# Local attention prepared two units earlier, and gated convolution as a rolling program over sequences

## The reference

```
xz = xn @ in_w.T + in_b
xi, z = jnp.split(xz, 2, axis=-1)
xc = conv1d(xi, conv_w, 4 taps, causal, one filter per feature) + conv_b
xc = _silu(xc)
xp = xc @ xproj_w.T
C = xp[..., 1 + D_STATE:]
gate = jax.nn.sigmoid(jnp.mean(C, axis=-1, keepdims=True))
y = xc * gate + D * xc
y = y * _silu(z)
y = y @ out_w.T + out_b
return y + residual
```

```
q, k, v = split(shift_token(x) @ wqkv)          # to heads
q = l2norm(q) * qs;  k = l2norm(k) * ksc
q, k = rotary_xpos(q, k)
sim  = einsum('bhwid,bhwjd->bhwij', bq, bk)     # bk, bv: this window and the last
attn = softmax(where(mask, -max, sim))
out  = einsum('bhwij,bhwjd->bhwid', attn, bv)
x = x + o @ wo                                  # a gated feed-forward follows
```

## Time and profile before

| | |
|---|---|
| median of 3 runs | 8063.11 us (8062.08 to 8072.71) |
| the profiled execution | 8073.38 us, its span 8071.7 us |
| PE busy | 5969.8 us (74%) |
| DVE busy | 4107.3 us (51%) |
| ACT busy | 2971.3 us (37%) |
| POOL busy | 1953.7 us (24%) |
| gated convolution | about 800.6 to 1000.1 us of the span |
| local attention, four times | 5220.5 to 5702.5, 5800.6 to 6281.0, 6879.0 to 7366.0, 7465.5 to 7949.8 us |

### The profile page before, as it was taken

The page is one execution under the profiler, slowest core; times in us unless marked ns, Lnnn a source line. Parts: engine busy times, 40 slices in busy tenths (PEclk is TensorE's granted clock), DMA queues, the critical chain, the costliest instruction groups (busy, mean ns, idle before and its releaser), DMA issues. The chain is left out here.

```text
span 8071.7 us, 121471 instructions
## 1 busy us (share of the span) xinstructions
PE 5969.8 (74%) x45848; PEld 2884.3 (36%) x45848; DVE 4107.3 (51%) x6441; ACT 2971.3 (37%) x6472; POOL 1953.7 (24%) x1781
## 2 busy tenths in 40 slices
PE   5557567786768876666678999877777798678677
PEld 3445151114442222222234544434344333344343
DVE  4333435662427745888844444344444566444444
ACT  1002323553334541444311222345355355354453
POOL 0113032212142201444511000034143011341341
PEclk6558676887888888787785887889899888899888
DMA  1001012211121100000003221111111000110110
GB/s 44 4 30 51 14 62 68 65 49 64 48 62 43 37 16 14 0 0 0 0 7 64 52 52 44 26 41 38 31 40 38 9 1 1 47 40 15 51 39 23
DMA packets 261161, 268.98 MB, mean 33 GB/s; under 512 B 113600, under 2 KB 190656, under 8 KB 258688
## 3 DMA queue, kind: packets, MB, share of 16 engines
q1 hardware_dynamic: 250368, 240.26, 11.5%
q0 software_dynamic: 10240, 21.25, 0.8%
HBM read 122.59 MB, written 71.66 MB: 24 GB/s over the span
## 5 line engine op out<-in xcount | busy, mean ns | idle before, releaser
L2170 PE MATMUL ps<-s_l2b_hc,ident 128*128 128x512 f32 x512 | 361.4, 846 | 332.6 <-DVE s_l2b_hc L2333 332.6
L1942 DVE TENSOR_REDUCE s_l3l_negmax<-ps 128x4 f32<-128x512 f32 x256 | 175.0, 683 | 744.0 <-PE ps L1783 744.0
L2118 POOL TENSOR_TENSOR s_l2b_Bx<-s_l2b_du,s_l2b_B 128x512 f32<-128x512 f32 x256 | 406.5, 1610 | 473.3 <-ACT s_l2b_B L2240 410.4
L1873 ACT ACTIVATE s_l3l_probs<-ps,s_l3l_biases,s_l3l_q_inverse 128x128 f32<-128x128 f32 x1024 | 455.6, 462 | 55.7 <-DVE s_l3l_biases L1944 55.3
L2325 DVE TENSOR_TENSOR_SCAN s_l2b_state<-s_l2b_decay,s_l2b_Bx 128x512 f32<-128x512 f32 x256 | 389.9, 1562 | 154.6 <-ACT s_l2b_decay L2246 113.3
L1721 POOL TENSOR_TENSOR s_l3l_probs<-s_l3l_probs,s_l3l_inverse 128x512 f32<-128x512 f32 x256 | 266.9, 1043 | 830.5 <-DVE s_l3l_inverse L1923 830.3
L1745 PE MATMUL ps<-s_l3l_hs,s_l3l_wqk 128*128 128x512 f32 x512 | 305.0, 703 | 177.3 <-DVE s_l3l_prod L1897 95.5
L1057 DVE TENSOR_REDUCE s_L3a_negmax<-ps 128x1 f32<-128x128 f32 (+3 forms) x512 | 236.1, 488 | 362.0 <-PE ps L893 359.5
L638 DVE TENSOR_REDUCE s_L1a_negmax<-ps 128x1 f32<-128x512 f32 x512 | 316.5, 681 | 153.3 <-PE ps L501 152.6
L1035 ACT ACTIVATE s_L3a_pt<-ps 128x256 f32<-128x256 f32 (+3 forms) x512 | 195.3, 434 | 530.3 <-PE ps L893 528.5
L908 PE MATMUL ps<-ks,s_L3a_qs 40*128 40x256 f32 (+3 forms) x1024 | 360.2, 610 | 30.1 <-DVE s_L3a_kvsq L1072 16.5
(11 more groups left out here) (658 smaller groups left out, 13547.7 us busy)
## 6 DMA issues: line engine op xcount, KB each, us to landing
s_l3l_qk<-s_l3l_rope SPq DMA_DIRECT2D x1024, 64.0 KB
scratch_rope<-s_L3a_rope SPq DMA_DIRECT2D x32, 512.0 KB, 2.8
ks<-scratch_parts SPq DMA_DIRECT2D x384, 32.0 KB
s_L3a_qs<-scratch_rope SPq DMA_DIRECT2D x64, 128.0 KB
ks<-scratch_rope SPq DMA_DIRECT2D x64, 128.0 KB
s_L0e_slots<-scratch_sent SPq DMA_DIRECT2D x16, 396.0 KB, 5.9
s_L1e_slots<-scratch_sent SPq DMA_DIRECT2D x16, 396.0 KB, 6.3
scratch_square<-s_L1a_rows SPq DMA_DIRECT2D x24, 256.0 KB, 3.0
```

What stands on the lines that cost most here:

```text
L1873: act.activation(t["probs"][:, U % (LAG + 1), k, :], ps[:, U % 2, P * k:P * (k + 1)], ACT.Exp, bias=t["biases"][:, U % (LAG + 1), k:k + 1] ...
L2118: pool.tensor_tensor(t["Bx"][:, n % 2, k, :], t["du"][:, b % 2, k, :], t["B"][:, n % 2, :], ALU.mult).then_inc(s["bx_ready"], 1)
L2170: pe.matmul(ps[:, 4 + k, :], g["ident"][:, :], t["hc"][:, n % 2, k, :], start=(n == 0), stop=(n == STATES - 1)).then_inc(s["summed"], 1)
```

## The change

Two stages are rewritten, the rest is as it was.

**Local attention.** The preparation runs two units earlier (`EARLY = 2`): units 0 to 5 of sequence b take what units 2 to 7 took, and units 6 and 7 take the first two items' units of sequence b+2. Before the first scores, the whole first sequence and two units of the second are prepared (`FIRST`). Two v items change places (the third v now comes with the norms). The signal of the DMAs is split in two, `q_stacked` and `k_stacked`, so that POOL waits only for the half whose rows it overwrites.

```
+    EARLY = 2
     def prep(b, u):
-        if b == BATCH:
+        if not 0 <= b < BATCH:
             return []
...
         if u == 4:
-            return [("norm", b), ("v", b, 1)]
+            return [("norm", b), ("v", b, 3)]
         if u == 5:
-            return [("v", b, 0), ("v", b, 3)]
+            return [("v", b, 0), ("v", b, 1)]
...
+    def beside(b, u):
+        u += EARLY
+        return prep(b + 1 + u // UNITS, u % UNITS)
+    FIRST = [item for u in range(UNITS) for item in prep(0, u)] + [item for u in range(EARLY) for item in prep(1, u)]
...
-                sp.wait_ge(s["stacked"], START + b * STACKED)
+                sp.wait_ge(s["q_stacked"], START + b * STACKED)
+                sp.wait_ge(s["k_stacked"], START + b * STACKED)
...
-                pool.wait_ge(s["stacked"], START + b * STACKED)
+                pool.wait_ge(s["q_stacked" if e < 2 else "k_stacked"], START + b * STACKED)
...
-                    if u < 4 and b + 1 < BATCH:
-                        rotate(b + 1, u)
-                    if u == 4 and b + 2 < BATCH:
+                    for ahead, e in ((b + 1, u + EARLY), (b + 2, u + EARLY - UNITS)):
+                        if 0 <= e < 4 and ahead < BATCH:
+                            rotate(ahead, e)
+                    if u == 3 and b + 2 < BATCH:
                         shift(b + 2)
```

```
+            for b in range(BATCH):                                     # POOL
+                pool.tensor_tensor(x[:, cols], x[:, cols], h[:, cols], ALU.add).then_inc(s["added"], 1)
...
+            for b in range(BATCH):                                     # PE
+                gates(b)
+                if b + 2 < BATCH:
+                    project_x(b + 2)
+                if b:
+                    outputs(b - 1)
+                if b + 1 < BATCH:
+                    project_z(b + 1)
+            outputs(BATCH - 1)
...
+            pad(0); pad(1); gate_rows(0)                               # ACT
+            for b in range(BATCH):
+                for k in range(2):
+                    act.activation(t["xc"][:, b % 2, k, :], t["conv"][:, b % 2, k, :], ACT.Silu).then_inc(s["xc_ready"], 1)
+                act.activation(t["gate"][:, b % 2, :], ps[:, 6, :], ACT.Tanh).then_inc(s["gate_ready"], 1)
+                if b + 2 < BATCH:
+                    pad(b + 2)
+                if b + 1 < BATCH:
+                    gate_rows(b + 1)
...
+            convolution(0)                                             # DVE
+            vec.tensor_copy(t["gate_w"][:, :, :], ps[:, 7, 0:2 * P].rearrange("p (k c) -> p k c", k=2)).then_inc(s["gate_copied"], 1)
+            for b in range(BATCH):
+                if b + 1 < BATCH:
+                    convolution(b + 1)
+                gated(b)
+                if b:
+                    add_out(b - 1)
+            add_out(BATCH - 1)
```

More of the change, by code:

```diff
@@ L1431, in gated_convolution @@
 def gated_convolution(nc, g, w):
[L1434 to L1437, removed]
@@ new lines, in outputs @@
+            def outputs(b):
+                pe.wait_ge(s["halved"], START + 1)
+                pe.wait_ge(s["done"], START + b)
+                for k in range(2):
+                    pe.wait_ge(s["y_ready"], START + 2 * b + k + 1)
+                    mm = pe.matmul(ps[:, 7, :], t["out_w"][:, k, :], t["y"][:, b % 2, k, :], start=(k == 0), stop=(k == 1))
+                mm.then_inc(s["out_ready"], 1)
+            project_x(0)
+            for k in range(2):
+                mm = pe.transpose(ps[0:16, 6, k * P:(k + 1) * P], t["c_w"][:, k, :], g["ident"][:, :])
@@ new lines, in _ @@
+            mm.then_inc(s["c_turned"], 1)
+            project_x(1)
+            pe.wait_ge(s["rows_copied"], START + 1)
+            pe.wait_ge(s["pads_set"], START + 1)
+            for k in range(2):
+                mm = pe.matmul(ps[:, 7, k * P:(k + 1) * P], t["c_rows"][:, k, :], t["thirty_second"][:, :], start=True, stop=True)
+            mm.then_inc(s["gate_made"], 1)
+            project_z(0)
+            pe.wait_ge(s["gate_copied"], START + 1)
+            for b in range(BATCH):
[6 more added lines that the diff above has]
+                    project_z(b + 1)
@@ L1516, in _, with gated @@
-                            own(ins, *((s["conv_done"], b * 2 + k + 1) if tap == 3 else ()))
+                            ins = vec.scalar_tensor_tensor(out=conv, in0=shifted, scalar=weight, in1=conv, op0=ALU.mult, op1=ALU.add)
+                            own(ins, *((s["conv_done"], 2 * b + k + 1) if tap == 3 else ()))
+            def gated(b):
                 vec.wait_ge(s["gate_ready"], START + b + 1)
+                if b > 1:
+                    vec.wait_ge(s["out_ready"], START + b - 1)
@@ L1713, in _ @@
             shift(1)
+            for e in range(EARLY):
+                rotate(1, e)
             shift_values(0)
@@ L1811, in values @@
                 mm.then_inc(s["pv_done"], 1)
-            for u in range(UNITS):
-                for item in prep(0, u):
-                    side(item)
+            for item in FIRST:
+                side(item)
             for U in range(BATCH * UNITS + BEHIND):
@@ L1826, in _ @@
                 if b < BATCH:
-                    for item in prep(b + 1, u):
+                    for item in beside(b, u):
                         side(item)
```

139 lines of the change are left out of this document (73 added, 66 removed).

## The result

The changed kernel takes 7727.1 us (median of 4 runs, 7723.0 to 7739.2) against 8067.9 us for the kernel before: a ratio of 0.9578, interval 0.956 to 0.9595, so 341 us less. 7694 was forecast, in a range of 7640 to 7790. The direction and the two main mechanisms came as forecast, but the gain fell some 30 us short, and one of its two parts fell short by more than that. One run of a later kernel (8154.3 us, of the one with the old way to the gate) fell into a slower state of the chip and is left out of its median.

A forecast was written before the change was run, and what follows sets the result against it. The gated convolution was taken as one chain with no engine full, the local attention as pausing for keys. Savings of 108 and 261 us, together 369, from 8063 gave 7694 us, range 7640 to 7790.

The forecast's parts named there:

- the third rival: Gated convolution: PE falls to its low clock level, 7726 us instead of 7694; chance 0.09.
- Rivals four and five: Local attention: denser work gets the low clock, 8179 us, chance 0.02; the keys' wait stays whole, 7955 us, chance 0.03.
- rival one: Local attention: part of the wait for keys stays; with half of it left 7806 us; chance 0.08.
- I take 0.6: Local attention: delay per sequence from POOL's shifted values standing ahead of the next unit's scaling, 0.6 us, bounds 0 and 3.35.
- The second rival: Local attention: POOL's queue becomes the wait, 3.35 us instead of 0.6 on 28 boundaries, 7771 us; chance 0.07.
- instead of 56.0 ... at each of seven boundaries: Local attention: a sequence takes 47.1 us instead of 56.0, saving 8.9 at each of seven boundaries, 62 us a stage.
- my 9.5: Local attention, unit 3, with the output projection and two v: priced at 9.5 us, at most the old 10.05.
- 47.1: Local attention: forecast time of one sequence in us, from units summing to 46.5 plus 0.6 for POOL.
- where 3 were expected: Local attention, seventh sequence: units 6 and 7 carry no projection, giving some 3 us more, limited by the keys.
- The keys' margin: Local attention: keys land 16.3 us after the unit with the picks starts, 2.5 us before units 4 to 7 end.
- The split of the signal: Local attention: splitting the signal lets POOL overwrite query rows in unit 6 while keys are still read; no separate size.

The follow-up runs named there:

- the old way to the gate: Changed kernel with the rolling gated convolution, but 16-row projection, ACT copy, mean by second matmul and sigmoid instead of combined matrix and tanh: 7744.4 us.
- The filler run: Changed kernel with POOL's shifted-value copies moved to units 5 and 6, and POOL writing zeros twice in their old place: 7738.1 us, ratio 0.9601.
- the copies in four pieces: Changed kernel with POOL's shifted-value copies made in four smaller pieces, two behind the scaling of unit 4 and two behind unit 5's: 7678.9 us, ratio 0.9517.
- the run with one unit: Changed kernel with the local attention's preparation moved one unit earlier instead of two (`EARLY = 1`): 7866.8 us, ratio 0.9754.
- the probe's stage: Changed kernel with a short stage at its start setting one small DVE instruction beside one POOL instruction at a time; no kernel time given.

## Why the prediction came out as it did

**Gated convolution: right.** 111 us against 108. DVE bounds, at 9.33 us a sequence instead of 9.8: a convolution takes 5.88 of it (I had 6.1), the four products 2.79 (2.9), the addition from PSUM 0.66 to the next start (0.75). PE was granted 0.90 over the stage and 1.00 from 840 to 880 us, the high level as chosen, so the third rival did not come. POOL's additions cost little: they hold DVE's doubling of D for 4.78 us, but the first convolution starts 10.65 us after the stage's own loads begin, against 9.9 before, where a few tenths were forecast.

**Local attention: right in kind, mis-sized.** The pause for the keys is gone at six of seven boundaries, the second to seventh sequences last 48.1 us on average, and no granted clock in a stage is below 0.92. Rivals four and five did not come, and rival one only at the seventh boundary. The 48 us that are missing in four stages have two main sources.

The larger is the term "I take 0.6" for POOL's shifted values. It measured 2.4 us (1.8 in unit 1, 0.6 in unit 2): 1.8 more in each of 24 sequences is 43 us. The step behind it was wrong as well. I asked only who is queued behind POOL's copies, and took bounds of 0 and 3.35 from that. The runs show that what counts is what DVE does while they last. The filler run shows that lateness alone leaves unit 1 as priced (5.91 in the eight sequences that test it); the copies in four pieces restore all three units to 5.80, 5.91 and 6.45. The second rival (7771) had the right place and the wrong mechanism.

The smaller is the base: "instead of 56.0 ... at each of seven boundaries" took the one sequence of the earlier trace rows for all. The 28 first to seventh sequences of the kernel before average 55.0 us (the first of a stage, without an output projection, 49.7 to 53.6), 28 us less in sum. Against these two, unit 3 was 0.64 shorter than my 9.5 (15 us back), and the first sequence came shorter than 47.1 for the same lack of an output projection (43.6 on average, 14 us back). The seventh sequence is 1.8 us shorter than those ahead of it, where 3 were expected: it is limited by the keys, as I wrote, and waits 3.4 to 3.8 us for them.

**The keys' margin** of 2.5 us was optimistic: 1.3, by the run with one unit. **The split of the signal**, which I named as a condition, is none. The 10 us in stages that the change does not touch lie within the spread of executions: they took 5888 to 5910 us in the traces of the eleven other kernels than that with the probe's stage, and the kernel before ran from 8046 to 8082 us in these comparisons.

## What to carry to other kernels

When a step is moved on one engine, ask not only who queues behind it, but what the engine that shares its access to SBUF does in that time: look for instructions there that read two SBUF tiles, or copy or scale one, above all tiny ones on the critical path. Such a stall shows as a long duration and not as idle time, so compare the longest instruction of a line with its median. And price a sequence by the mean over all its repetitions; the first and last of a pipeline differ from the one in the middle.

## What the hardware showed that I had not expected

The Trainium skill, "SBUF — State Buffer", section "🔬 SBUF: two separate sides", says that VectorE and GpSimd share a pair of SBUF ports by an exclusive lock: a DVE instruction with two SBUF inputs (against a GpSimd instruction that reads SBUF) or in a two-port mode, or the GpSimd instruction, whichever starts first, holds it to its end. I had not weighed it. The probe agrees: 1.45 to 1.54 us for 128x4 numbers beside POOL's 1.89 us copy, and 0.15 to 0.21 with an input from PSUM. The filler agrees as well: under POOL's writes of zeros, which read nothing, the bias product takes 0.17 us.

One number goes beyond a single instruction. In the changed kernel's gated convolution DVE's multiply-add of 128 x 2 numbers started at 816.23 beside eight POOL additions of 1.25 us that have no wait between them, and it got through only after the last of them, three instruction borders later (the last six additions in one row):

```profile
813.63 7.35 POOL L1454 TENSOR_TENSOR x_res<-x_res,h 128x512 f32<-128x512 f32 x6
...
816.23 4.78 DVE L1550 TENSOR_SCALAR s_l0b_D<-s_l0b_D 128x2 f32<-128x2 f32 x1 [6.19 <-DMA s_l0b_out_b<-in_L0b_out_b_dram]
```

Behind a copy that POOL follows with a wait of its own, the bias product got in between the two copies: in the rows of unit 1 above, the first copy ends at 7443.60, the product at 7443.62, and the second copy starts at 7443.66.
